# A graph-attention stage: the column groups of its weighted sum take halves of the queries in place of even and odd key blocks

## The chip, the cores and the metric

One core of a Trainium2 chip runs the whole program; seven others are idle. The metric is the device time of one execution in microseconds (us), the median of the executions. Engines: TensorE (PE, its weight loads are listed apart as PEld), VectorE (DVE), ScalarE (ACT), GpSimd (POOL), SyncE (SP, which here only issues DMA).

## What is computed

Four graph layers follow each other on x of 8 graphs x 1024 nodes x 64 features, each behind a layer norm. The change lies in the fourth, and there in its hidden attention:

```
def gat_layer(x, graph, W, b):
    h = x @ W                                  # one head: 64 -> 128
    s = einsum('bnd,bmd->bnm', h, h) * graph
    s = where(s == 0.0, -1e16, s)
    a = softmax(s, axis=2)
    return einsum('bnm,bmd->bnd', a, h) + b
heads = vmap(...)                              # 8 heads
x = leaky_relu(cat(heads), 0.01)               # 8 x 128 = 1024 channels
out = gat_layer(x, graph, W_out, b_out)
```

All is float32. With 8 graphs and 8 heads there are 64 units of work; a unit is one head of one graph. In a unit the kernel uses that a @ (x W) = (a @ x) W: it sums the 64 input features of the keys with the softmax weights (this is z, 64 features for each of 1024 queries), divides by the row sums, and multiplies by the head's W (64 to 128) and by its part of W_out (128 to 64) afterwards.

## The kernel before

`hidden_attention` (L275 to L718) runs for each unit g over 8 tiles t of 128 queries x 1024 keys. The order of each engine is written out by hand in one loop for each engine over g and t; semaphores tie them.

For a tile: PE makes the scores (`score`, L411, four products of 512 columns in a two-pass format), DVE adds the mask and takes the row maximum (`mask_tile`, L547), ACT takes the exponential and the row sum in place (`exp_tile`, L628), DVE turns the tile in 32 x 32 blocks into `weights_t` (`turn_tile`, L556). The scores have two places in PSUM, so `score(i)` waits until tile i - 2 is masked (`masked_ready`); step t of unit g issues the score of tile 8g + t + 2. The ring behind them holds four tiles.

After a unit's eight tiles are turned, its results are made while the next unit's tiles run:

- `values(g-1, part)` (L425), in four parts, at t = 2, 3, 4, 5, behind the score of that step. The keys stand in 32 blocks of 32 (NB = 32, Q = 32). `x_rep` holds the features of a key block repeated on the four groups of 32 partitions, and `weights_t` has, on each group a of 32 partitions, the weights of 256 queries. A product therefore uses 32 rows and 64 columns of the array: row group a of four, and column group c of two. Before the change c = b % 2: even key blocks are summed on partitions 0 to 63 of PSUM and odd ones on 64 to 127, in products of 256 columns; a part is 8 key blocks x 4 row groups = 32 products. A float32 product appears in the profile as two records, each with a weight load of its own, so a part is 64 records.
- `copy_z` (L632, ACT, t = 6) moves the sums out of PSUM as z, 128 x 1024: two half sums, still to be added.
- `normalise` (L693, POOL) multiplies z in place by the inverse row sums `inv_cols`. These come from `invert` (DVE, t = 1), go through memory (`inv_rows`) and come back spread over 128 partitions, in two DMAs on SP (L373, L377).
- `head_out` (L444, PE, t = 0 of the unit after) multiplies by `wz`. Its two products (one for each half of the queries, 512 columns, 128 rows) also add the even and odd sums, since `wz` stands twice, on rows 0 to 63 and 64 to 127. They are four records.
- `activate` (L639, ACT, t = 0, behind `exp_tile` and `copy_y`), then `project_out` (L451, PE, t = 1): `wo` x hidden and `wx` x z, for the two halves of the queries in the two column groups, eight records. `take_out` (ACT) and `add_out` (POOL) follow.

`project(g+2)` (L403), `copy_y`, `round_y` and `split_y` prepare the factor y of the scores of a later unit. Some units have further work on DVE: of each graph's eight units u = 0 to 7, u = 1 and 2 end with `split_rows` (L521), u = 3 and 4 with `find_zero_cols` (L530), both for the next graph, and u = 7 builds its mask (L537, eight times). The last graph has none of it.

## Time and profile before

| | us |
|---|---|
| median of 3 runs | 2781.16 |
| lowest, highest | 2780.2, 2785.39 |
| profiled execution, its time | 2786.11 |
| profiled execution, its span | 2784.3 |
| of it the hidden attention's 64 units, with their tail | about 996 to 2491 |

The profiled execution lies 5 us above the median; 1.8 us lie around its span. Durations below are those of this one execution. A row with "x64" stands for 64 instructions; in rows of the timeline the columns are start, duration, engine, line, operation, output<-input, count, and in brackets how long the engine had been idle and what ended that. PE durations are modelled and include the way through the array, so that two neighbours overlap; the distance between starts is the better measure.

### The profile page before, as it was taken

Reading aid. Unit: us, or ns where it says so; the run is one execution under the profiler, and the core shown is the slowest. Engines: PE = TensorE matmul, PEld = TensorE weight load, DVE = VectorE, ACT = ScalarE, POOL = GpSimd, SP = SyncE. Lnnn points to the kernel's source line nnn. Section 1 sums busy time; section 2 is a strip of 40 time slices with the busy share of each in tenths; the row PEclk is TensorE's granted clock in tenths of the full one; section 3 lists DMA queues with packets and bytes.
Section 4 is the critical chain, followed back from the end, with each engine's and each line's share of the span. In section 5 each row is a group of like instructions: output and inputs, shape, how many; then the busy total and the mean of one; then the engine's idle time right before and its main releaser. Section 6 shows DMA issues by size and latency. Waiting matters only on the chain. (4 is left out here: it accounts for less than half of the span.)

```text
span 2784.3 us, 57963 instructions
## 1 busy us (share of the span) xinstructions
PE 2259.4 (81%) x24510; PEld 1463.7 (53%) x24510; DVE 2234.9 (80%) x2971; ACT 1471.3 (53%) x2331; POOL 602.4 (22%) x351
## 2 busy tenths in 40 slices
PE   3855556667767689999999898998998989968997
PEld 2632234444446555565555555655555556636665
DVE  6569985678874598988988989989889898837775
ACT  2412221369962156566566665665656656636665
POOL 0036662000000012222222222222222222210000
PEclk8968788879988779999999999999999999979999
DMA  2000000000000201010010010100100100010000
GB/s 104 1 0 0 0 0 0 2 1 1 1 2 1 59 23 39 17 47 25 24 40 25 27 38 17 48 25 25 40 25 28 36 17 32 25 47 1 1 1 31
DMA packets 61879, 60.79 MB, mean 22 GB/s; under 512 B 50368, under 2 KB 51520, under 8 KB 60992
## 3 DMA queue, kind: packets, MB, share of 16 engines
q1 hardware_dynamic: 61632, 57.21, 6.6%
q8 instruction: 191, 3.13, 0.5%
q14 instruction: 56, 0.46, 0.1%
HBM read 44.34 MB, written 4.46 MB: 18 GB/s over the span
## 5 line engine op out<-in xcount | busy, mean ns | idle before, releaser
L547 DVE CUSTOM_DVE_ANT_0 x_sb<-ps_score,hid_mask 128x1024 f32<-128x1024 f32 x512 | 616.5, 1204 | 142.4 <-PE ps_score L419 140.3
L628 ACT ACTIVATE x_sb<-x_sb,hid_neg_max 128x1024 f32<-128x1024 f32 x512 | 586.8, 1147 | 268.2 <-DVE hid_neg_max L547 268.1
L556 DVE STREAM_TRANSPOSE hid_weights_t<-x_sb 128x1024 f32<-128x1024 f32 x512 | 631.4, 1233 | 1.3 <-ACT x_sb L628 0.6
L419 PE MATMUL ps_score<-hid_y_hi,hid_xs 128*128 128x512 f32 x1024 | 471.4, 460 | 51.3 <-DVE hid_neg_max L547 47.8
L437 PE MATMUL ps_low<-hid_weights_t,hid_x_rep 32*64 32x256 f32 x16384 | 506.7, 380 | 0.8 <-ACT hid_share L656 0.8
L437 PEld LDWEIGHTS ps_low<-hid_weights_t,hid_x_rep 32*64 32x64 f32 x16384 | 346.2, 131 | 139.9 <-issue 82.3
L419 PE MATMUL ps_score<-hid_y_lo,hid_xs 128*128 128x512 f32 x1024 | 411.2, 402 | 0.0
L697 POOL TENSOR_TENSOR hid_z<-hid_z,hid_inv_cols 128x1024 f32<-128x1024 f32 x64 | 197.9, 3092 | 761.1 <-ACT hid_z L636 761.1
L419 PEld LDWEIGHTS ps_score<-hid_y_hi,hid_xs 128*128 128x128 f32 x1024 | 195.6, 191 | 257.5 <-issue 116.0
L690 POOL TENSOR_TENSOR hid_y_lo<-hid_y_wide,hid_y_hi 128x1024 fp32r<-128x1024 f32 x64 | 153.1, 2392 | 348.5 <-ACT hid_y_wide L623 348.5
L419 PEld LDWEIGHTS ps_score<-hid_y_lo,hid_xs 128*128 128x128 f32 x1024 | 197.1, 192 | 42.9 <-issue 14.6
L447 PE MATMUL ps_low<-hid_z,hid_wz 128*128 128x512 f32 x256 | 134.0, 648 | 38.1 <-POOL hid_z L697 22.2
L636 ACT COPY hid_z<-ps_low 128x1024 f32<-128x1024 f32 x64 | 64.8, 1012 | 143.0 <-PE ps_low L437 143.0
L1788 ACT ACTIVATE hyp_blend_exp<-hyp_blend,hyp_minus_one 128x512 f32<-128x512 f32 x72 | 52.0, 723 | 161.7 <-DVE hyp_blend L1851 161.7
L167 PE MATMUL ps_low<-ident,gat_weights 128*128 128x128 f32 x512 | 80.0, 307 | 61.7 <-ACT gat_weights_t L256 55.6
L537 DVE SCALAR_TENSOR_TENSOR hid_mask<-hid_zero_col,hid_zero_row,adj_mask 128x1024 bf16<-128x1024 bf16 x64 | 111.3, 1748 | 0.0
L167 PEld LDWEIGHTS ps_low<-ident,gat_weights 128*128 128x128 f32 x512 | 64.1, 157 | 85.9 <-issue 43.2
L219 DVE CUSTOM_DVE_ANT_0 out_masked<-ps_score,out_mask 128x1024 f32<-128x1024 f32 x64 | 78.3, 1224 | 27.6 <-issue 22.9
L708 POOL TENSOR_TENSOR h_sb<-h_sb,hid_share 128x512 f32<-128x512 f32 x56 | 72.0, 1285 | 131.4 <-ACT hid_share L656 131.4
L447 PEld LDWEIGHTS ps_low<-hid_z,hid_wz 128*128 128x128 f32 x256 | 46.9, 201 | 97.0 <-POOL hid_z L697 34.5
L643 ACT ACTIVATE hid_hidden<-ps_low,hid_bias_pos 128x1024 f32<-128x1024 f32 x64 | 71.4, 1116 | 49.7 <-PE ps_low L447 48.8
L618 ACT CAST hid_y_hi<-ps_low 128x1024 fp32r<-128x1024 f32 x64 | 65.0, 1016 | 61.8 <-PE ps_low L406 61.8
(308 smaller groups left out, 3810.5 us busy)
## 6 DMA issues: line engine op xcount, KB each, us to landing
hid_inv_cols<-hid_inv_rows SPq DMA_DIRECT2D x64, 512.0 KB, 3.7
hid_x_rep<-h_sb SPq DMA_DIRECT2D x128, 64.0 KB, 2.5
adj_rows<-in_adj SPq DMA_DIRECT2D x8, 512.0 KB, 8.0
x_sb<-in_x SPq DMA_DIRECT2D x2, 1024.0 KB, 6.1
x_saved<-x_sb SPq DMA_DIRECT2D x1, 2048.0 KB, 6.5
x_sb<-x_saved SPq DMA_DIRECT2D x1, 2048.0 KB, 8.0
out_x<-x_sb SPq DMA_DIRECT2D x1, 2048.0 KB, 6.3
hid_inv_rows<-hid_row_inv SPq DMA_DIRECT2D x64, 4.0 KB, 1.4
```

Source lines behind the costliest of these rows:

```text
L167: ins = pe.transpose(m.ps_turn[:, half, k * P:(k + 1) * P], a.weights[:, t % 3, j * P:(j + 1) * P], m.ident[:])
L219: dve.tensor_tensor_reduce(a.masked[:, t % 2, :], scores, mask, -1.0, HUGE, ALU.add, ALU.min, a.neg_max[:, par, t:t + 1]).then_inc(a.maske ...
L419: ins = pe.matmul(m.ps_score[:, i % 2, half * HALF:(half + 1) * HALF], xs[:, g // HEADS % 2, t * P:(t + 1) * P], y[g % 2][k][:, half * HAL ...
L437: ins = pe.matmul(m.ps_low[c * F:(c + 1) * F, a, 0:NT * Q], x_rep[a * Q:(a + 1) * Q, g // HEADS % 2, b, :], weights_t[a * Q:(a + 1) * Q, g ...
L447: ins = pe.matmul(m.ps_low[:, half, :], wz[:, g % HEADS, :], z[:, half * HALF:(half + 1) * HALF], start=True, stop=True)
L537: dve.scalar_tensor_tensor(out=mask[:, t, :], in0=zero_col[:], scalar=zero_row[:, t:t + 1], in1=m.mask[:, t, :], op0=ALU.min, op1=ALU.min) ...
L547: dve.tensor_tensor_reduce(ring[:, i % RING, :], m.ps_score[:, i % 2, :], mask[:, t, :], -1.0, HUGE, ALU.add, ALU.min, neg_max[:, g % 2, t ...
L556: dve.transpose(weights_t[:, g % 2, :, t, :], ring[:, i % RING, :].rearrange("p (b j) -> p b j", j=Q)).then_inc(tile_turned, 1)
L628: act.activation(ring[:, i % RING, :], ring[:, i % RING, :], ACT.Exp, scale=-1.0, bias=neg_max[:, g % 2, t:t + 1], accum_out=row_sum[:, g ...
L690: pool.tensor_tensor(y[g % 2][1][:], y_wide[:], y[g % 2][0][:], ALU.subtract)\
L697: pool.tensor_tensor(rows, rows, inv_cols[:].rearrange("p i t -> p t i"), ALU.mult)\
L708: pool.tensor_tensor(out, out, share[:].rearrange("p (t f) -> p t f", f=F), ALU.add)\
```

## The change

The column group c no longer takes every other key block but one half of the queries that a row group holds: 128 of its 256 columns. Each key block is now multiplied twice, with c = 0 and c = 1, in products of 128 columns, and each accumulates over all 32 key blocks. A part has 64 products (128 records, each with its weight load) in place of 32 (64 records). z then is 128 x 512: partitions 0 to 63 hold the first 512 queries and 64 to 127 the others, and nothing remains to be added. So `copy_z` and `normalise` handle half the elements, `inv_cols` is half as large and filled by two DMAs of 64 partitions, `head_out` and the `wx` products of `project_out` use 64 rows for each half of the queries in place of 128.

```diff
-        inv_cols = sb("inv_cols", [P, P, NT])
-        z = sb("z", [P, N])
+        inv_cols = sb("inv_cols", [P, P, NT // 2])
+        z = sb("z", [P, HALF])
...
-                sp.dma_start(inv_rows[g % 2], row_inv[:, g % 2, :]).then_inc(inv_stored, 16)
+                sp.dma_start(inv_rows[g % 2].rearrange("c p t -> p c t"),
+                             row_inv[:, g % 2, :].rearrange("p (c t) -> p c t", c=2)).then_inc(inv_stored, 16)
...
-                sp.dma_start(inv_cols[:].rearrange("p i t -> p (i t)"),
-                             inv_rows[g % 2].rearrange("(a p) t -> a (p t)", a=1).to_broadcast([P, N]))\
-                    .then_inc(inv_spread, 16)
+                for c in range(2):
+                    sp.dma_start(inv_cols[c * F:(c + 1) * F, :, :].rearrange("p i t -> p (i t)"),
+                                 inv_rows[g % 2, c:c + 1].rearrange("a p t -> a (p t)")
+                                 .to_broadcast([F, HALF])).then_inc(inv_spread, 16)
...
                 for b in range(part * NB // 4, (part + 1) * NB // 4):
-                    c = b % 2
                     for a in range(P // Q):
-                        ins = pe.matmul(m.ps_low[c * F:(c + 1) * F, a, 0:NT * Q],
-                                        x_rep[a * Q:(a + 1) * Q, g // HEADS % 2, b, :],
-                                        weights_t[a * Q:(a + 1) * Q, g % 2, b, :, :],
-                                        start=(b == c), stop=(b == NB - 2 + c))
+                        for c in range(2):
+                            ins = pe.matmul(m.ps_low[c * F:(c + 1) * F, a, 0:NT // 2 * Q],
+                                            x_rep[a * Q:(a + 1) * Q, g // HEADS % 2, b, :],
+                                            weights_t[a * Q:(a + 1) * Q, g % 2, b,
+                                                      c * NT // 2:(c + 1) * NT // 2, :],
+                                            start=(b == 0), stop=(b == NB - 1))
...
                 for half in range(2):
-                    ins = pe.matmul(m.ps_low[:, half, :], wz[:, g % HEADS, :],
-                                    z[:, half * HALF:(half + 1) * HALF], start=True, stop=True)
+                    rows = slice(half * F, (half + 1) * F)
+                    ins = pe.matmul(m.ps_low[:, half, :], wz[rows, g % HEADS, :], z[rows, :],
+                                    start=True, stop=True)
...
-                for k, (weight, src) in enumerate(((wo, hidden), (wx, z))):
-                    for half in range(2):
-                        ins = pe.matmul(m.ps_low[half * F:(half + 1) * F, 0, :], weight[:, g % HEADS, :],
-                                        src[:, half * HALF:(half + 1) * HALF],
-                                        start=(k == 0), stop=(k == 1))
+                for half in range(2):
+                    pe.matmul(m.ps_low[half * F:(half + 1) * F, 0, :], wo[:, g % HEADS, :],
+                              hidden[:, half * HALF:(half + 1) * HALF], start=True, stop=False)
+                for half in range(2):
+                    rows = slice(half * F, (half + 1) * F)
+                    ins = pe.matmul(m.ps_low[rows, 0, :], wx[rows, g % HEADS, :], z[rows, :],
+                                    start=False, stop=True)
...
-                act.copy(z[:].rearrange("p (t a j) -> p a t j", t=NT, a=P // Q),
-                         m.ps_low[:, :, 0:NT * Q].rearrange("p a (t j) -> p a t j", j=Q)).then_inc(z_ready, 1)
+                act.copy(z[:].rearrange("p (t a j) -> p a t j", t=NT // 2, a=P // Q),
+                         m.ps_low[:, :, 0:NT // 2 * Q].rearrange("p a (t j) -> p a t j", j=Q))\
+                   .then_inc(z_ready, 1)
...
-                rows = z[:].rearrange("p (t i) -> p t i", t=NT)
+                rows = z[:].rearrange("p (t i) -> p t i", t=NT // 2)
                 pool.tensor_tensor(rows, rows, inv_cols[:].rearrange("p i t -> p t i"), ALU.mult)\
                     .then_inc(z_normed, 1)
```

No instruction changes its place among the others of its engine. On PE, a stretch with two parts of the weighted sum (`ps_low<-hid_weights_t`) between the scores of two tiles reads, before the change:

```order
L437 MATMUL ps_low<-hid_weights_t,hid_x_rep 64x256 x32
L419 MATMUL ps_score<-hid_y_hi,hid_xs 128x512
L419 MATMUL ps_score<-hid_y_lo,hid_xs 128x512
L419 MATMUL ps_score<-hid_y_hi,hid_xs 128x512
L419 MATMUL ps_score<-hid_y_lo,hid_xs 128x512
L437 MATMUL ps_low<-hid_weights_t,hid_x_rep 64x256 x32
```

and with the change, where line 437 has become 439 and line 419 has become 421:

```order
L439 MATMUL ps_low<-hid_weights_t,hid_x_rep 64x128 x64
L421 MATMUL ps_score<-hid_y_hi,hid_xs 128x512
L421 MATMUL ps_score<-hid_y_lo,hid_xs 128x512
L421 MATMUL ps_score<-hid_y_hi,hid_xs 128x512
L421 MATMUL ps_score<-hid_y_lo,hid_xs 128x512
L439 MATMUL ps_low<-hid_weights_t,hid_x_rep 64x128 x64
```

The products of a part have doubled in number and halved in columns; what stands around them is the same.

## Rows read from the trace of the kernel before

**Rows 1.** The page: busy time of each engine, share of the span, instructions.
```profile
PE 2259.4 (81%) x24510; PEld 1463.7 (53%) x24510; DVE 2234.9 (80%) x2971; ACT 1471.3 (53%) x2331; POOL 602.4 (22%) x351
```

**Rows 2.** Waits from 996 to 2457 us: who waited for whom, total, times, longest.
```profile
DVE x_sb L547 <- PE ps_score L419: 140.3, 241, 1.1
...
PEld ps_low L447 <- POOL hid_z L697: 25.4, 27, 1.1
```

**Rows 3.** Timeline: two steps with a part of the weighted sum.
```profile
1603.04 0.40 PE L419 MATMUL ps_score<-hid_y_lo,hid_xs 128*128 128x512 f32 x1
1603.36 1.53 PEld L437 LDWEIGHTS ps_low<-hid_weights_t,hid_x_rep 32*64 32x64 f32 x64 [0.36 <-issue]
1603.37 1.98 PE L437 MATMUL ps_low<-hid_weights_t,hid_x_rep 32*64 32x256 f32 x64
1603.47 1.22 DVE L547 CUSTOM_DVE_ANT_0 x_sb<-ps_score,hid_mask 128x1024 f32<-128x1024 f32 x1 [0.65 <-PE ps_score L419]
...
1606.40 1.98 PE L437 MATMUL ps_low<-hid_weights_t,hid_x_rep 32*64 32x256 f32 x64
```

**Rows 4.** Short stretches of one part, line 437: length, PE busy (records in it), clock, DMA.
```profile
1600.32:1600.38 0.06, 0.06 (x8) 1.00 0.73 158
1600.38:1600.59 0.21, 0.21 (x8) 1.00 0.97 235
1600.59:1600.65 0.06, 0.06 (x16) 1.00 1.27 337
```

**Rows 5.** Timeline and line 393: 128-column products in two column groups.
```profile
1609.56 1.09 PE L393 MATMUL ps_low<-ident,h_sb 128*64 128x128 f32 x16
...
L393 PE MATMUL ps_low<-ident,h_sb x256: 272/273/475, 974.5 to 2166.2; 128*64 128x128 f32 x128
```

**Rows 6.** Groups by line and shape: busy us, mean ns, idle before and its releasers.
```profile
L697 POOL TENSOR_TENSOR hid_z<-hid_z,hid_inv_cols 128x1024 f32<-128x1024 f32 x64 | 197.9, 3092 | 761.1 <-ACT hid_z L636 761.1
L447 PE MATMUL ps_low<-hid_z,hid_wz 128*128 128x512 f32 x256 | 134.0, 648 | 38.1 <-POOL hid_z L697 22.2 <-DVE hid_zero_col L530 12.9 <-DVE hid_xs L521 3.1
L636 ACT COPY hid_z<-ps_low 128x1024 f32<-128x1024 f32 x64 | 64.8, 1012 | 143.0 <-PE ps_low L437 143.0
L656 ACT COPY hid_share<-ps_low 128x512 f32<-128x512 f32 x56 | 32.9, 587 | 57.8 <-PE ps_low L455 57.8
L708 POOL TENSOR_TENSOR h_sb<-h_sb,hid_share 128x512 f32<-128x512 f32 x56 | 72.0, 1285 | 131.4 <-ACT hid_share L656 131.4
```

**Rows 7.** Timeline around head_out and activate, a unit with split_rows before it.
```profile
1614.82 1.00 ACT L623 COPY hid_y_wide<-ps_low 128x1024 f32<-128x1024 f32 x1
...
1615.88 1.12 ACT L643 ACTIVATE hid_hidden<-ps_low,hid_bias_pos 128x1024 f32<-128x1024 f32 x1
```

**Rows 8.** The same with find_zero_cols before it.
```profile
1636.48 1.98 PE L447 MATMUL ps_low<-hid_z,hid_wz 128*128 128x512 f32 x4 [0.92 <-DVE hid_zero_col L530]
...
1638.50 1.12 ACT L643 ACTIVATE hid_hidden<-ps_low,hid_bias_pos 128x1024 f32<-128x1024 f32 x1 [0.76 <-PE ps_low L447]
...
1642.77 1.22 DVE L547 CUSTOM_DVE_ANT_0 x_sb<-ps_score,hid_mask 128x1024 f32<-128x1024 f32 x1 [0.57 <-PE ps_score L419]
```

**Rows 9.** The same in a unit with neither.
```profile
2376.41 1.12 ACT L643 ACTIVATE hid_hidden<-ps_low,hid_bias_pos 128x1024 f32<-128x1024 f32 x1 [0.33 <-PE ps_low L447]
```

**Rows 10.** Timeline of the tail, from the last turned tile on.
```profile
2457.77 2.85 POOL L697 TENSOR_TENSOR hid_z<-hid_z,hid_inv_cols 128x1024 f32<-128x1024 f32 x1 [11.38 <-ACT hid_z L636]
...
2460.68 2.71 PE L447 MATMUL ps_low<-hid_z,hid_wz 128*128 128x512 f32 x4 [4.10 <-POOL hid_z L697]
...
2463.43 1.11 ACT L643 ACTIVATE hid_hidden<-ps_low,hid_bias_pos 128x1024 f32<-128x1024 f32 x1 [4.60 <-PE ps_low L447]
...
2480.31 3.78 PE L447 MATMUL ps_low<-hid_z,hid_wz 128*128 128x512 f32 x4 [4.08 <-POOL hid_z L697]
```

**Rows 11.** PE in stretches of the tail: busy (records), granted clock, DMA.
```profile
2461.00:2465.00 4.00, 2.80 (x6) 0.60 0.43 132
...
2481.00:2485.00 4.00, 3.09 (x4) 0.50 0.00 0
```

More of the change, by code:

```diff
@@ L311, in hidden_attention @@
         share = sb("share", [P, HALF])
-        inv_rows = nc.dram_tensor("hid_inv_rows", (2, P, NT), F32).ap()
+        inv_rows = nc.dram_tensor("hid_inv_rows", (2, 2, P, NT // 2), F32).ap()
         gram_ready = sem("gram_ready")
@@ L383, in _ @@
                     load_rows(g // HEADS + 1)
-            sp.wait_ge(inv_spread, 16 * UNITS)
+            sp.wait_ge(inv_spread, 32 * UNITS)
         @block.tensor
@@ L694, in normalise @@
                 pool.wait_ge(z_ready, g + 1)
-                pool.wait_ge(inv_spread, 16 * (g + 1))
-                rows = z[:].rearrange("p (t i) -> p t i", t=NT)
+                pool.wait_ge(inv_spread, 32 * (g + 1))
+                rows = z[:].rearrange("p (t i) -> p t i", t=NT // 2)
                 pool.tensor_tensor(rows, rows, inv_cols[:].rearrange("p i t -> p t i"), ALU.mult)\
```

## The prediction

> **What bounds the kernel now.** The page first: PE and DVE are each busy four fifths of the span, ACT and POOL far less [rows 1]. So the question in each stretch is which of PE and DVE waits for the other. The list of waits answers it for the 64 units: DVE waited for scores 241 times, 140 us in all, 0.58 us each [rows 2]. The timeline shows where: in the four steps that carry a part of the weighted sum, the step takes 3.04 us (1603.37 to 1606.40), PE has no pause in it beyond the change of product kind, and DVE sits idle 0.65 us before each mask [rows 3]. In these steps PE sets the time, in all others DVE does. The exception are the eight units that build masks (u = 7) and half of those behind them, where DVE has work enough everywhere. So 241 steps of 512 are PE's, and there a nanosecond more or less in a part is one on the path.
>
> The start of this PE-bound stretch is set by another chain: z is normalised, head_out, activate, project_out, then the score of t = 2 and the first part. Every nanosecond by which project_out ends earlier moves the whole PE-bound stretch, since DVE idles in it.
>
> **Values (the heart of it).** How PE runs a part now: eight records start within 0.06 us, none in the next 0.21 us, then eight more (the count in the next stretch goes to 16, since the first eight still flow), and so on [rows 4]. Eight are the eight combinations of row and column group; they stream side by side, and a new eight comes when they are through, every 0.216 us (1.98 less one duration of 0.374 is 1.61 us, for seven such steps, the first weight load and 0.05 us from first to last of eight [rows 3]). With 128 columns: line 393 has products of 128 columns in two column groups, 16 records in 1.09 us; less one duration of 0.273 and the first load of 0.05, that is 0.77 us for seven steps of a pair, 0.109 us each [rows 5]. So a step of half the columns takes half the time, and its weight load still hides behind the record before it. A part of the changed kernel has 128 records, 16 steps of eight: 15 x 0.109 + 0.10 = 1.74 us to its last start, and that record then streams 0.107 in place of 0.213 us. Now 1.61 + 0.21 = 1.82, then 1.74 + 0.11 = 1.85: I take **+0.02 us** a part, and 241 x 0.02 = **+5 us**. Bounds: what this needs is a record each 13.6 ns over 1.7 us. The trace shows eight within 0.06 us (7 ns each, so one engine start is no limit) but never more than 64 in 1.7 us (27 ns each). From below, the two steps cannot be shorter than their columns: -0.02, -5 us. From above, 27 ns each would be 3.46 us a part, +1.6 us, +390 us. I take the low end, because the 27 ns have a cause in the rows: eight records start at once and then nothing starts for 0.21 us, which is waiting for the columns and not for records; and the pairs of line 393 halve their step when the columns halve.
>
> The Trainium skill's page "TensorE: Matmul & The Clock Gate" (section "Wait — 56ns, not 53.3ns?") says that start-to-start never drops below about 25 ns however small the product is. By that a part would take 128 x 25 ns = 3.2 us, an estimate from the page, and the kernel would come out some 330 us slower. Against it stand the eight starts in 0.06 us in different groups of the array; for it, that no row has sustained more than one in 27 ns.
>
> **The rest of z.** copy_z writes 512 elements a partition in place of 1024: 1.01 us becomes 0.59 (line 656, same shape) [rows 6]. normalise: 3.09 becomes about 1.5; line 708 with 512 elements takes 1.29, which is the floor [rows 6]. head_out: four records of 512 columns follow each other, 0.43 us each (1.98 us with a duration of 0.59 and a load of 0.1) [rows 8]; with 64 rows each, the two halves lie in different row groups and run side by side, as the four row groups of a part do, so 4 x 0.43 becomes 2 x 0.43, **-0.86 us**. project_out: wo is unchanged; the wx pair ran in two column groups and still does, so two steps remain two steps. What is new is a change of the array's division in the middle. Its price from a row: the last score record starts at 1603.04 and streams 0.23 us (the distance of such records), so it is through at 1603.27; the first load of the part stands at 1603.36, and 0.05 us more go to that load, which is not ahead of time [rows 3]. So **+0.14 us**, on the path, between 0 and 0.2. The Trainium skill's page "TensorEngine Tiling (Array Packing)" (section "Key Properties") says that changing the tiling mode drains the engine, and the row agrees with 0.09 us of pause.
>
> What of this reaches the end depends on activate, which on ACT stands behind copy_y and waits for head_out. Three kinds of unit:
> - With split_rows before it: activate starts 0.06 us after copy_y, without a wait [rows 7]. Nothing is gained; the 0.14 us are lost. 7 graphs x 2 = 14 units: **+2.0 us**.
> - With find_zero_cols before it: head_out starts late for DVE's sake (0.92 us, in total 12.9, hence 14 times [rows 6, 8]), activate waits 0.76 us for it, and 0.06 of that remains behind copy_y. 0.70 - 0.14 = 0.56 us, x 14 = **-7.9 us**.
> - With neither: head_out waits for normalise (27 times [rows 2]), activate waits 0.33 us [rows 9]. normalise and copy_z together are 2 us earlier, so head_out starts with its score, and ends early: 0.27 - 0.14 = 0.13 us. Of the 27, seven are in the mask-building units, where DVE hides it. 20 x 0.13 = **-2.6 us**.
> The gain is at most what DVE idles at t = 2 and after (0.57 and 4 x 0.65 us [rows 8, 3]), so all of it counts.
>
> **The tail.** Behind the last tile everything is one chain, twice: copy_z, normalise, head_out, activate, project_out [rows 10]. Each time copy_z gives 0.43 and normalise 2.85 / 2 = 1.42 us. The first head_out takes 2.75 us (2460.68 to 2463.43) because the granted clock drops in it (mean 0.60, between full and half [rows 11]); 1.85 us earlier it lies before the drop and has half the steps: about 1.05, -1.7 us. The second runs at half clock (0.50, that is 1.2 GHz): four steps of 0.85 become two, -1.7. Less two changes of division, 0.2 each: 2 x 1.85 + 3.4 - 0.4 = **-6.7 us**. Between -4.5 and -8.5, by where the clock falls.
>
> **Without effect.** The two DMAs that fill inv_cols carry half the bytes each and are issued one behind the other on SP, where nothing waits behind them but the loads of the next graph's rows; normalise sat idle 11 to 12 us before copy_z ended and never waited for inv_cols (all 761 us of its wait are copy_z's [rows 6]). If the smaller pieces of the store cost even 3 us it is hidden. PE's program grows by 64 x 4 x 128 instructions; were its supply late, that would be the first rival.
>
> **Sum.** +5.0 + 2.0 - 7.9 - 2.6 - 6.7 = -10.2 us against the span of 2784.3: 2774.1. The profiled execution (2786.1) lies 5 us over the median, so it goes on the median: 2781.2 - 10.2 = **2771.0 us**, 0.4% faster. What a measurement of this kernel can tell from no change is about 0.2%, 5.6 us.
>
> **Rivals.**
> 1. *Records come too slowly* (slower). The engine can't sustain a record with its load each 13.6 ns. From 13.6 ns on each nanosecond costs 128 ns a part, 31 us over 241 parts. At 17 ns: 0.44 us a part, +100 us, 2870; at the 27 ns that are all that was ever sustained: +390 us, 3160. For it: never seen. Against it: rows 4 and 5 as above. Chance 0.14, most of it at the mild end.
> 2. *The row groups open one after another* (slower). The new order puts both halves of a row group (four records) in front of the next one. If PE takes records strictly in order and the second record of one group blocks those behind it, a key block costs 4 x (0.109 + 0.013) = 0.49 in place of 0.218 us, a part 3.9 us, +2.1 us, +500 us, 3270. Against it: eight starts in 0.06 us [rows 4] can only be, with two records to each product, if records pass waiting ones even now. Chance 0.06.
> 3. *It comes to nothing* (within 0.2%). The parts lose 0.04 us in place of 0.02, the division changes cost 0.2 in head_out too, and the tail's clock falls elsewhere: -10.2 + 5 + 3 + 2 = 0, 2781. Each of the three is within its bounds. Chance 0.20.
> 4. *My forecast*, -6 to -20 us: 0.60. The far end is parts at -0.02 us.
>
> Chances: faster 0.60, same 0.20, slower 0.20. The range 2760 to 2798 takes in forecast and rival 3, and of rival 1 what costs up to 17 us (14.1 ns a record); outside lie about 0.2.
>
> **What would show it.** In the changed kernel's timeline: a part of 128 records in 1.95 us, the step still 3.05 us, DVE idle 0.65 us in it. Rival 1 shows a part of 2.2 to 3.5 us, DVE idle 1 us and more; rival 2 one of 4 us. L447 successor: four records, two and two, 1.1 us from first start to last end in place of 1.98. Its wait for POOL is gone. activate's wait of 0.76 and 0.33 us is gone. project_out ends 0.14 us later behind activate. The tail (2457 to 2490) is 6 us shorter. I am wrong in the main thing if the parts change by more than 0.05 us either way.

## The result, and the profile after

The changed kernel takes 2899.11 us (median of 4), the kernel before 2783.27 us in the same comparison: 1.0415 times as long, interval 1.0395 to 1.0435. The prediction was 2771 us, faster; even its range, up to 2798, is missed by 100 us. The profiled execution has a span of 2896.5 us, 112.2 more than before. In this comparison and in those below every execution lies close to its median except one: one of the six of e13 took 6441 us, and its ratio leaves that one out.

The page of the changed kernel: busy times, and the queue that brings instructions.

```profile
PE 2299.6 (79%) x40894; PEld 1574.0 (54%) x40894; DVE 2221.2 (77%) x2971; ACT 1441.7 (50%) x2331; POOL 503.4 (17%) x351
...
q8 instruction: 319, 5.23, 0.8%
```

The same queue on the page of the kernel before (packets, MB, share of 16 DMA engines):

```profile
q8 instruction: 191, 3.13, 0.5%
```

PE's busy time grew by 40 us only [rows 1], though it has 32,768 more instructions (records and loads). They come in 128 more packets of 16 KB, so a packet holds 256 instructions.

The waits of the changed kernel (total, times, longest), against 140.3 us in 241 times of [rows 2]; the second row is PE's loads in the parts waiting for nothing that a semaphore shows:

```profile
DVE x_sb L553 <- PE ps_score L421: 251.4, 207, 3.4
...
PEld ps_low L439 <- issue: 181.0, 403, 2.2
```

The timeline, the first three parts of one unit, to be laid beside [rows 3]:

```profile
1714.69 2.10 PE L439 MATMUL ps_low<-hid_weights_t,hid_x_rep 32*64 32x128 f32 x128
...
1717.84 0.67 PE L439 MATMUL ps_low<-hid_weights_t,hid_x_rep 32*64 32x128 f32 x27
...
1719.35 1.77 PE L439 MATMUL ps_low<-hid_weights_t,hid_x_rep 32*64 32x128 f32 x101 [0.84 <-issue]
...
1722.17 0.66 PE L439 MATMUL ps_low<-hid_weights_t,hid_x_rep 32*64 32x128 f32 x23
...
1722.28 1.23 DVE L553 CUSTOM_DVE_ANT_0 x_sb<-ps_score,hid_mask 128x1024 f32<-128x1024 f32 x1 [1.94 <-PE ps_score L421]
...
1723.09 1.81 PE L439 MATMUL ps_low<-hid_weights_t,hid_x_rep 32*64 32x128 f32 x105 [0.27 <-issue]
```

Here are both causes of the loss. The first part is whole: 2.10 us against 1.98, its step 3.15 us against 3.04. The second breaks off after 27 records; for 0.8 us PE has nothing in flight and waits for nobody ("issue"), then come the other 101. The third breaks after 23. From here on, "first to last" means from the start of a part's first record to the start of its last, and a hole is a distance of over 0.3 us between two starts in a part. All 252 parts of the kernel before take 1.61 us first to last, without a hole. In the changed kernel a part that nothing holds up takes 1.83 us (68 of them), and 126 of 252 have a hole (87 us in all, the longest 2.7); the mean is 2.29 us.

The start of the whole part, in short stretches (length, PE busy and records in flight in it, then loads, clock, DMA), beside [rows 4]:

```profile
1714.69:1714.80 0.11, 0.11 (x8) 0.11 (x16) 1.00 0.37 11
1714.80:1714.91 0.11, 0.11 (x16) 0.11 (x24) 1.00 0.85 24
...
1716.00:1716.20 0.20, 0.20 (x34) 0.20 (x26) 1.00 0.00 0
```

In it four groups of eight start as forecast (the last three 0.109 us apart, within a group 6.7 ns from record to record); after these come mostly single starts, about 16.5 ns apart, in two streams that overlap.

The groups of the z side and of the masks (busy, mean ns, idle before), beside [rows 6]:

```profile
L704 POOL TENSOR_TENSOR hid_z<-hid_z,hid_inv_cols 128x512 f32<-128x512 f32 x64 | 99.3, 1552 | 880.1 <-ACT hid_z L642 880.1
...
L451 PE MATMUL ps_low<-hid_z,hid_wz 64*128 64x512 f32 x256 | 74.2, 657 | 26.6 <-DVE hid_zero_col L536 17.4 <-DVE hid_xs L527 4.6 <-POOL hid_z L704 4.6
...
L642 ACT COPY hid_z<-ps_low 128x512 f32<-128x512 f32 x64 | 37.5, 586 | 229.2 <-PE ps_low L439 228.9
```

They do what was forecast: normalise goes from 3.09 to 1.55 us, copy_z from 1.01 to 0.59, and head_out's four records take 1.13 us in place of 1.98; head_out waits for POOL 5 us in all, no longer 22.

The clearest rows stand in the tail, where the last unit's whole sum runs with no scores between (before: 256 records in one piece, 7.17 us):

```profile
2575.80 2.42 PE L439 MATMUL ps_low<-hid_weights_t,hid_x_rep 32*64 32x128 f32 x151 [0.78 <-ACT hid_share L663]
2579.88 2.08 PE L439 MATMUL ps_low<-hid_weights_t,hid_x_rep 32*64 32x128 f32 x128 [1.66 <-issue]
2583.90 3.01 PE L439 MATMUL ps_low<-hid_weights_t,hid_x_rep 32*64 32x128 f32 x128 [1.94 <-issue]
2587.64 3.27 PE L439 MATMUL ps_low<-hid_weights_t,hid_x_rep 32*64 32x128 f32 x105 [0.73 <-issue]
2590.98 0.58 ACT L642 COPY hid_z<-ps_low 128x512 f32<-128x512 f32 x1 [15.32 <-PE ps_low L439]
```

The pieces break off 128 records apart: 128 records with their 128 loads are one packet of 256 instructions. The packets' work starts 4.0 and 3.7 us apart. Between 1000 and 2400 us of the changed kernel the two closest instruction packets start 3.28 us apart; a step with a part wants a little more than one (264 instructions) and should take 3.05 us.

The trace shows the same in the middle of the kernel. If all PE instructions in it (82,345) are numbered in the order of their starts, every one of the 129 holes (126 in parts, three in the tail) ends at the 137th or 138th of a block of 256, that is always at the same place of a packet; so do all holes of e1, e3, e6, e11 and e14 (29 to 141 in each). A packet's own record ends 1.2 to 1.6 us before the hole does (nine in ten, median 1.40). And in 47 of the 48 units outside u = 7 and 0 the first part, which follows four steps without a part, is whole: the same instructions run at full pace where the supply had time to get ahead.

### The profile page after: what moved, and what is told of

The parts are those of the page before. It is cut to its first block and busy times, and to the rows that moved or that the text cites. A ratio compares the mean times of both kernels' runs of the same rounds, so it can differ in the third digit from the quotient of the medians.

```text
span 2896.5 us, 90795 instructions
## 1 busy us (share of the span) xinstructions
PE 2299.6 (79%) x40894; PEld 1574.0 (54%) x40894; DVE 2221.2 (77%) x2971; ACT 1441.7 (50%) x2331; POOL 503.4 (17%) x351
## 5 line engine op out<-in xcount | busy, mean ns | idle before, releaser
L439 PE MATMUL ps_low<-hid_weights_t,hid_x_rep 32*64 32x128 f32 x32768 | 601.7, 276 | 59.7 <-issue 56.6
L439 PEld LDWEIGHTS ps_low<-hid_weights_t,hid_x_rep 32*64 32x64 f32 x32768 | 500.2, 131 | 189.4 <-issue 181.0
L421 PE MATMUL ps_score<-hid_y_hi,hid_xs 128*128 128x512 f32 x1024 | 449.9, 439 | 49.2 <-DVE hid_neg_max L553 42.3
L704 POOL TENSOR_TENSOR hid_z<-hid_z,hid_inv_cols 128x512 f32<-128x512 f32 x64 | 99.3, 1552 | 880.1 <-ACT hid_z L642 880.1
L642 ACT COPY hid_z<-ps_low 128x512 f32<-128x512 f32 x64 | 37.5, 586 | 229.2 <-PE ps_low L439 228.9
L167 PE MATMUL ps_low<-ident,gat_weights 128*128 128x128 f32 x512 | 79.8, 306 | 61.7 <-ACT gat_weights_t L256 55.6
L458 PE MATMUL ps_low<-hid_hidden,hid_wo 128*64 128x512 f32 x256 | 70.8, 632 | 40.7 <-ACT hid_hidden L650 39.5
L543 DVE SCALAR_TENSOR_TENSOR hid_mask<-hid_zero_col,hid_zero_row,adj_mask 128x1024 bf16<-128x1024 bf16 x64 | 100.4, 1577 | 0.0
L634 ACT ACTIVATION_READ_ACCUMULATOR x_sb<-x_sb,hid_neg_max 128x1 f32 x512 | 97.0, 189 | 0.0
L249 ACT ACTIVATE out_weights<-out_masked,out_neg_max 128x1024 f32<-128x1024 f32 x64 | 73.5, 1149 | 46.8 <-DVE out_neg_max L219 46.2
L451 PE MATMUL ps_low<-hid_z,hid_wz 64*128 64x512 f32 x256 | 74.2, 657 | 26.6 <-DVE hid_zero_col L536 17.4
```

The lines of the kernel that those rows point to most:

```text
L167: ins = pe.transpose(m.ps_turn[:, half, k * P:(k + 1) * P], a.weights[:, t % 3, j * P:(j + 1) * P], m.ident[:])
L249: act.activation(a.weights[:, t % 3, :], a.masked[:, t % 2, :], ACT.Exp, scale=-1.0, bias=a.neg_max[:, par, t:t + 1], accum_out=a.row_sum[ ...
L421: ins = pe.matmul(m.ps_score[:, i % 2, half * HALF:(half + 1) * HALF], xs[:, g // HEADS % 2, t * P:(t + 1) * P], y[g % 2][k][:, half * HAL ...
L439: ins = pe.matmul(m.ps_low[c * F:(c + 1) * F, a, 0:NT // 2 * Q], x_rep[a * Q:(a + 1) * Q, g // HEADS % 2, b, :], weights_t[a * Q:(a + 1) * ...
L451: ins = pe.matmul(m.ps_low[:, half, :], wz[rows, g % HEADS, :], z[rows, :], start=True, stop=True)
L543: dve.scalar_tensor_tensor(out=mask[:, t, :], in0=zero_col[:], scalar=zero_row[:, t:t + 1], in1=m.mask[:, t, :], op0=ALU.min, op1=ALU.min) ...
```

## Experiments

**Theory A**: PE's instructions arrive too slowly, one packet of 256 in 3.3 us or more, 13 ns an instruction. **Rivals**: B, the halves of 128 columns, their order or their number cost the array time; C, the columns or the array's handling of each record set it. As one measure for all, the stretch of a unit from the first record of its first part to the last start of its fourth (with three scores between; the mean over units, without those whose sum runs in u = 7 or 0): before, 536 PE instructions in 10.73 us; changed, 1048 in 13.23 us (11.67 to 16.18), 12.6 ns an instruction.

**Twice the records, nothing else (e1).** The kernel before, each product in two of 128 columns that follow in the same tile of the array.

```diff
-                        ins = pe.matmul(m.ps_low[c * F:(c + 1) * F, a, 0:NT * Q], ...)
+                        for s in range(2):
+                            ins = pe.matmul(m.ps_low[c * F:(c + 1) * F, a, s * NT // 2 * Q:(s + 1) * NT // 2 * Q], ...)
...
```

> The kernel before, with each product of the weighted sum issued as two products of 128 columns of the same column group: records and weight loads as many as in the changed kernel, everything else (z of full size, key blocks even and odd) as before. Theory A, instruction supply: blocks of 16 KB (256 instructions) reach PE no faster than one in about 3.3 us, and a step with a part now needs 264 and more; holes of 0.3 to 2 us with nothing issued appear in the parts, as in the changed kernel, and the time is that of the changed kernel plus what the smaller z gives, 2899 + 8 to 14 = 2905 to 2920 us. Rival B, the order of the row groups or the query halves are at fault: no holes, 2780 to 2800 us.

2995.76 us, ratio 1.0751 (1.0733 to 1.0769). Twice the records are enough to do the damage, but not as expected, and both theories missed the time: the clean part is 2.55 us, and only 30 parts have a hole (22 us). Stretch 14.61 us: 13.9 ns an instruction, so the supply nearly follows. An added record costs (2.55 - 1.61) / 64 = 14.7 ns here, against 3.4 in the changed kernel. Here four records in a row go to one tile (one row group with one column group), there two; whether that order is the reason was not shown, and e11 below, whose added records change tile, pays about as much.

**The smaller z with the long products (e2).** The changed kernel, but each key block as before in one product of 256 columns, even and odd blocks apart; their addition is left out.

```diff
+                    c = b % 2
-                        for c in range(2):
-                            ins = pe.matmul(m.ps_low[c * F:(c + 1) * F, a, 0:NT // 2 * Q], ...)
+                        ins = pe.matmul(m.ps_low[c * F:(c + 1) * F, a, 0:NT * Q], ...)
```

> The changed kernel with the products of the kernel before (256 columns, even and odd key blocks); the adding of even and odd sums is left out, and z, normalise, head_out and wx handle half of it. It shows what the smaller z gives by itself. My sum of the prediction without the parts: -2.0 ... that is +2.0 - 7.9 - 2.6 - 6.7 = -15 us, so 2768 us; the parts as before (64 records in 1.98 us). Rival: project_out's two kinds of product cost more than head_out gives, 2780 us or above.

2756.38 us, 0.9895 (0.9878 to 0.9911); span 31.0 us less than before. Parts as before. So z gives 31 us, twice my sum, and what the 64 more records a part cost is 112.2 + 31.0 = 143 us.

**The order (e3).** The changed kernel, column groups outside and row groups inside, as the eight of the kernel before.

```diff
-                    for a in range(P // Q):
-                        for c in range(2):
+                    for c in range(2):
+                        for a in range(P // Q):
```

> The changed kernel with the loops over row group and column group exchanged (four row groups of one column group, then four of the other), the same products. Theory A, instruction supply: within 0.5% of the changed kernel, 2885 to 2913 us, with the same holes. Rival B, two products of one row group in a row hold up those behind them: parts as short as 1.95 us and 2780 to 2800 us.

2907.19 us, 1.0442 (1.0424 to 1.0459), an interval that overlaps the changed kernel's: no gain. Clean part 1.83 us, holes in 138 parts. The order of the row groups is not the cause.

**Empty instructions (e5).** The kernel before with four nops behind each product, each raising a semaphore.

```diff
+                        for filler in fillers:
+                            pe.nop().then_inc(filler, 1)
```

> The kernel before with four empty PE instructions (each only counts up a semaphore of its own) behind each product of the weighted sum: as many instructions as in the changed kernel, but products, columns and weight loads as before. Theory A, instruction supply: the holes appear all the same, 2880 to 2920 us. Rival C, what limits is the array's handling of records and weight loads, not the number of instructions: at most a few ns for each, no holes, 2785 to 2800 us.

7206.17 us, 2.5869 times, far outside both expectations. In the timeline the next product starts only when the records before the nops have about ended; 32,768 nops cost 4420 us, 135 ns each, with the granted clock down to 0.63 on average. Packets then come 17 us apart and more: the run says nothing on the supply.

**An eighth of the columns (e9).** The number of instructions is kept and the array's work taken away.

```diff
-                            ins = pe.matmul(m.ps_low[c * F:(c + 1) * F, a, 0:NT // 2 * Q],
+                            tiles = NT // 2 if b == 0 else 1
+                            cols = Q if b == 0 else 16
+                            ins = pe.matmul(m.ps_low[c * F:(c + 1) * F, a, 0:tiles * cols],
...
```

> The changed kernel with the same 128 records a part (the same number of PE instructions), but each product of a key block other than the first streams 16 columns in place of 128; the weighted sum of the other columns is left out. So the array has an eighth of the work. Theory A (PE's instructions come too slowly: blocks of 256 instructions, never closer than about 3.3 us in the changed kernel's trace, so some 13 ns an instruction): the step with a part has 264 to 270 instructions and still takes 3.4 us and more on average, holes with nothing issued stay in the parts, and the time is 2820 to 2880 us, near the 2899 of the changed kernel. Rival B (each record start costs PE its 14 to 17 ns, and the holes belong to the products in the array): clean parts of about 1.8 us remain, the holes go, 2750 to 2780 us. Rival C (columns set all of it): a part takes under 1 us, DVE never waits for scores, 2620 to 2660 us.

3005.91 us, 1.079 (1.0744 to 1.0836): outside every expectation, not under the changed kernel but above it, because the granted clock fell (mean 0.79 against 0.92), which lengthens the scores. The stretch is 13.50 us (11.69 to 16.16) against the changed kernel's 13.23, but the two can't be compared: the changed kernel's ran at full clock, these at a mean of 0.63 to 0.91, where a step without a hole takes up to 3.91 us, 2.63 at full clock. What can be compared are the holes: 105 parts have them, 119 us in all. Timeline:

```profile
2613.26 1.75 PE L441 MATMUL ps_low<-hid_weights_t,hid_x_rep 32*64 32x16 f32 x128
2616.06 0.30 PE L441 MATMUL ps_low<-hid_weights_t,hid_x_rep 32*64 32x16 f32 x6
2617.40 1.38 PE L441 MATMUL ps_low<-hid_weights_t,hid_x_rep 32*64 32x16 f32 x122 [1.04 <-issue]
2619.84 0.39 PE L441 MATMUL ps_low<-hid_weights_t,hid_x_rep 32*64 32x16 f32 x2
2621.15 1.96 PE L441 MATMUL ps_low<-hid_weights_t,hid_x_rep 32*64 32x16 f32 x126 [0.92 <-issue]
```

The holes belong to the number of instructions, not to the array's work, and all but one of them end at the same place of a block of 256 as in the changed kernel. Rivals B and C fall for the holes. What stands of a price of the record itself: a whole part took 1.37 us at full clock (10.7 ns a record) and 1.72 at half.

**Half the records (e4).** The changed kernel with one 128-column product for each key block and row group; the other half of the columns is left out.

```diff
-                        for c in range(2):
+                    c = b % 2
```

> The changed kernel, but with one product for each key block and row group as in the kernel before (even blocks in one column group, odd ones in the other), of 128 in place of 256 columns; so 64 records a part, and half of the columns of the weighted sum is left out. Theory A (supply of instructions): a step with a part has some 200 instructions, 2.6 us of supply, less than DVE needs; no holes, the part takes about 0.9 us from first to last start (8 steps of 0.109 us), DVE does not wait for scores, 2610 to 2650 us. Rival B (128-column products in themselves start badly, whatever their number): parts of 1.3 us and more with holes, 2690 to 2760 us. Against the run with 128 records of 16 columns this one has eight times the columns a record and half the records.

2604.18 us, 0.9347 (0.9328 to 0.9365). (A step has 136 PE instructions; the expectation's 200 was miscounted.) Four parts have holes, 4 us; stretch 7.87 us. DVE's wait for scores is gone from the list. The same 128-column products, half as many, are harmless. Within a part they start as densely as in the changed kernel (64 in 0.94 us, 14.7 ns each), but a step of 2.27 us asks for 136 instructions, 16.7 ns each, in place of 264.

```profile
1697.50 1.21 PE L439 MATMUL ps_low<-hid_weights_t,hid_x_rep 32*64 32x128 f32 x64
...
1699.77 1.21 PE L439 MATMUL ps_low<-hid_weights_t,hid_x_rep 32*64 32x128 f32 x64
```

**Three quarters (e14).** The changed kernel with 96 records a part; a quarter of the keys is left out.

```diff
-                for b in range(part * NB // 4, (part + 1) * NB // 4):
+                for b in range(part * 6, (part + 1) * 6):
...
```

> The changed kernel with six key blocks a part in place of eight: 96 records in place of 128, 16 products of two 128-column halves left out of the weighted sum in each part (a quarter of the keys). From the first record of the first part to the last of the fourth there are 792 PE instructions in place of 1048. Theory A (a supply of 12.6 ns an instruction, which is what 1048 in 13.2 us were, with 128 columns as with 16): 792 x 12.6 = 10.0 us; the array alone needs 4 x 1.38 + 3 x 1.46 = 9.9. So holes are rare (under 30 parts, under 20 us in all) and the stretch takes 9.9 to 10.6 us, less than the 10.73 of the kernel before with 64 long records: 2700 to 2745 us. Rival (each 128-column record brings its share of the holes): 3/4 of 127 parts and of 92 us, 2760 to 2790 us.

2725.97 us, 0.9778 (0.9763 to 0.9792), as theory A says; stretch 10.36 us, inside its 9.9 to 10.6. Holes in 47 parts and 33 us, more than the 30 parts and 20 us it allowed, half of the rival's 95 parts and 69 us. So the limit sets in gradually: the shortest stretch (9.50 us) has 12.0 ns an instruction, the mean one 13.1, and a unit in which a packet comes late shows it. Its tail shows the same size of piece with another program:

```profile
2410.56 2.42 PE L439 MATMUL ps_low<-hid_weights_t,hid_x_rep 32*64 32x128 f32 x151 [0.78 <-ACT hid_share L663]
2414.12 2.08 PE L439 MATMUL ps_low<-hid_weights_t,hid_x_rep 32*64 32x128 f32 x128 [1.14 <-issue]
2417.87 1.81 PE L439 MATMUL ps_low<-hid_weights_t,hid_x_rep 32*64 32x128 f32 x105 [1.66 <-issue]
```

151 and 128 again, though its parts have 96 records: this program is shorter by 16,384 instructions, 64 whole packets, so the packets end at the same place of the last sum.

**Tiny records added to the kernel before (e11).**

```diff
...
+                    for k in (b - 1, b):
+                        for a in range(P // Q):
+                            ins = pe.matmul(m.ps_low[k % 2 * F:(k % 2 + 1) * F, a, 0:16], ...)
...
```

> The kernel before with its 64 records a part unchanged, and behind each two key blocks the same eight products once more with 16 of the 256 columns (these columns are then counted twice in the weighted sum). So the PE instructions of the changed kernel (128 records a part) come with the z side and the long products of the kernel before, and the array's work grows by 16 columns in 256, 6%. Theory A (supply): blocks of 256 instructions come no closer than 3.3 us, a step with a part has 264 instructions and more, so it takes 3.4 us on average in place of 3.04, with holes in a third to a half of the parts: 2870 to 2930 us, as the changed kernel plus its saving on z. Rival B (something in the two 128-column halves themselves, or in four records of one row group in a row): no holes, a part takes 1.61 us + 8 short steps of 0.05 to 0.1 us, +0.1 to +0.2 us in place of holes: 2810 to 2840 us.

2984.68 us, 1.072 (1.0704 to 1.0736): both theories missed. A clean part takes 2.60 us, not 1.7: eight long records and eight tiny ones take 0.325 us, eight long ones 0.216, so each added record costs (2.60 - 1.61) / 64 = 15.5 ns though it has 16 columns. At 13.9 ns an instruction (stretch 14.56 us) the supply nearly follows, and only 26 parts have holes (19 us). Theory A is thus not the whole: a second price is paid by the record itself, and here, as in e1, it hides the first.

**Five parts in place of four (e6 from the changed kernel, e7 from the one before).**

```diff
-                for b in range(part * NB // 4, (part + 1) * NB // 4):
+                for b in range(part * NB // 5, (part + 1) * NB // 5):
...
-                    if 2 <= t < 6 and 1 <= g <= UNITS:
+                    if 2 <= t < 7 and 1 <= g <= UNITS:
...
```

> The changed kernel with the weighted sum of a unit in five parts (behind the scores of t = 2 to 6, six or seven key blocks each) in place of four, and the turning of the next graph's rows behind the last part moved from t = 6 to t = 7. Theory A (supply): a step with a part has some 240 instructions, 3.15 us of supply, against 3.45 before; five such steps take 15.7 us where four and one without a part took 14.4 + 2.4 = 16.8; holes get rarer, DVE waits less; 60 units by 0.8 to 1.1 us: 2830 to 2860 us. Rival B (the holes belong to the array and come with each part, whatever stands around it): as many holes as before or more (five parts), and each clean step 2.8 us; 2860 to 2900 us.

> The kernel before with its weighted sum in five parts at t = 2 to 6 in the same way. A step with a part had 3.04 us and 0.65 us of DVE idle; with four fifths of a part it has 2.72 us (1.61 / 5 = 0.32 less), the fifth one in place of a 2.4 us step. Five of 2.72 and none of 2.4: 13.6 against 4 x 3.04 + 2.4 = 14.6 us, 1.0 us a unit by some 55 units: 2725 to 2740 us if the longer way of z (its last part is one tile later) is hidden; 2760 to 2790 if head_out then comes late. Theory A adds: some 187 instructions a step, no holes in either case.

e6: 2869.23 us, 1.0308 (1.0289 to 1.0327). The holes fell from 87 to 54 us, in 83 of 314 parts, as a thinner stream of instructions (200 to 232 a step; the 240 written there was too many) lets the supply follow more often. e7: 2823.3 us, 1.0133 (1.0113 to 1.0153), slower where I expected faster. The fifth part ends a tile later and z with it; `head_out` waits for POOL 36 times, 55.6 us, with the score of t = 1 behind it: DVE idles 0.9 to 1.4 us before that tile's mask in u = 1, 4, 5 and 6, where it did not idle before. **e8** (from e7) and **e10** (from e6) were to move ACT's copy of z out of the way:

```diff
...
+                    if t == 7 and 1 <= g <= UNITS:
+                        copy_z(g - 1)
                     if g < UNITS:
                         exp_tile(g * NT + t)
...
-                    if t == 6 and 1 <= g <= UNITS:
-                        copy_z(g - 1)
-                    if t == 6 and n < B and u in (1, 2):
+                    if t == 7 and n < B and u in (1, 2):
```

> The kernel before with the weighted sum in five parts, and ACT's copy of z (and its rounding of the next rows) moved from behind exp of t = 6 to ahead of exp of t = 7, so that ACT no longer waits for the fifth part (it waited 295 us for it against 143 with four). Theory (the loss of 38 us was ACT's wait): DVE idles 0.33 us in five steps in place of 0.65 in four, less what PE waits for z's copy in t = 7: 2745 to 2775 us. Rival (z's way is one tile longer whatever ACT does, and PE's project and turning of rows stand behind it): 2790 to 2830 us.

> The changed kernel with the weighted sum in five parts and ACT's copy of z moved in the same way. Against the version with five parts without that move (2869 us) it should give back what ACT waits: if that is as in the kernel before, 30 to 50 us, 2820 to 2840. The holes of a slow instruction supply stay as they are with five parts (60 us in 109 parts), so theory A expects it to stay above the kernel before; if it falls under 2786 the supply would not be what holds the change back.

2816.86 (1.0119) and 2861.18 us (1.0289). The edit was a slip: behind exp of t = 6 and ahead of exp of t = 7 are the same place in ACT's order, so only the rounding of the rows moved. ACT waited 294.7 us for the fifth part as in e7 (294.6). Neither theory was tested; that an extra part can pay with z's way shortened stays open.

**Where do z's 31 us come from? (e12)** Unit by unit (each from its mask of t = 2 to the next unit's), e2 against before: u = 2, 3 with split_rows ahead -2.6 us in all (forecast +2), u = 4, 5 with find_zero_cols ahead -10.5 (forecast -7.9), u = 1 and 6 -4.6 (forecast -2.6), the two chains of the tail -5.7 (forecast -6.7), u = 0 +2.5, and u = 7, of which I said "DVE hides it", -8.9. (How much falls to u = 0 and how much to u = 7 depends on where a unit is said to begin; their sum is -6 to -9.) In u = 7 of the kernel before, in the timeline of POOL and DVE:

```profile
1147.70 2.38 POOL L690 TENSOR_TENSOR hid_y_lo<-hid_y_wide,hid_y_hi 128x1024 fp32r<-128x1024 f32 x1 [1.77 <-ACT hid_y_wide L623]
...
1148.45 2.72 DVE L537 SCALAR_TENSOR_TENSOR hid_mask<-hid_zero_col,hid_zero_row,adj_mask 128x1024 bf16<-128x1024 bf16 x1
...
1163.88 1.27 DVE L537 SCALAR_TENSOR_TENSOR hid_mask<-hid_zero_col,hid_zero_row,adj_mask 128x1024 bf16<-128x1024 bf16 x1
...
1166.20 2.95 POOL L697 TENSOR_TENSOR hid_z<-hid_z,hid_inv_cols 128x1024 f32<-128x1024 f32 x1 [13.09 <-ACT hid_z L636]
...
1167.35 2.88 DVE L537 SCALAR_TENSOR_TENSOR hid_mask<-hid_zero_col,hid_zero_row,adj_mask 128x1024 bf16<-128x1024 bf16 x1
```

A building of the mask takes 1.27 us, but where POOL is at work it ends 1.1 us behind the end of POOL's instruction (1150.08 and 1151.17; 1169.15 and 1170.23): it waits for it. All 22 buildings that start under an instruction of POOL end 1.08 or 1.09 us behind it, whether they take 2.3 or 3.4 us. e12 halves normalise alone:

```diff
-                rows = z[:].rearrange("p (t i) -> p t i", t=NT)
+                rows = z[:].rearrange("p (t i) -> p t i", t=NT)[:, 0:NT // 2, :]
```

> The kernel before, but POOL normalises only the first 512 of z's 1024 columns (the division by the row sum is left out for the others); all else is as before. Theory (POOL's normalise disturbs DVE's building of the mask where they fall together: 2.8 us in place of 1.27 for one of the eight in 7 of the graphs): one building of a mask in each u = 7 takes 1.27 us, 7 x 1.4 = -9.8 us; in the tail 2 x 1.6 = -3.1; units where head_out waited for POOL 0 to -0.3 us each: in all -13 to -20 us, 2762 to 2770. Rival (those instructions are slow for a reason of their own, and the 30 us of the smaller z came from copy_z or head_out): -3 to -8 us, 2773 to 2780.

2767.81 us, 0.9949 (0.9934 to 0.9965), in the theory's range. The instruction that took 2.88 us takes 1.45; normalise alone brings 15 us, about half of z's gain. The Trainium skill's page "SBUF — State Buffer" (section "Who interferes with whom") says that a DVE instruction with two SBUF inputs and a GpSimd instruction that reads SBUF lock each other out for the whole instruction, whichever came first. The rows agree where POOL's instruction came first, and DVE's mask_tile, whose one input is in PSUM, keeps its 1.20 us beside POOL. POOL waiting for DVE is not shown.

**The masks moved out of the way (e13).** The kernel before with nothing left out of it; only the place of the buildings changes.

```diff
                     if n < B and u == HEADS - 1:
-                        build_mask(n, t)
+                        for k in {2: (0, 1), 3: (2, 3), 4: (4, 5), 6: (6, 7)}.get(t, ()):
+                            dve.wait_ge(masked_ready, g * NT + k + 1)
+                            build_mask(n, k)
```

> The kernel before; only the eight buildings of the next graph's mask on DVE in u = 7 are issued at other steps: two each behind the masks of t = 2, 3, 4 and 6 in place of one in each step, so that none falls on POOL's split_y (t = 0 and 7) and normalise (t = 5). Theory (a building of the mask waits for POOL's instruction to end before it starts: 2.72 of which 1.64 overlap, 2.88 of which 1.79, 2.28 of which 1.20, against 1.27 alone): up to 1.5 + 1.6 + 1.0 = 4.1 us in 7 graphs, 29 us; as the moved ones may meet POOL's other work in one or two places, 2755 to 2770 us. Rival (PE or ACT holds u = 7 as soon as DVE is faster, or the POOL work moves along with it): 2775 to 2785 us.

2766.70 us, 0.9930 (0.9917 to 0.9943): 0.7% faster than the kernel before and 4.6% faster than the changed one, in the theory's range. All 56 moved buildings now take 1.3 us, what they take alone; of the 64 in the row (busy us, mean ns) only one of the first graph, which did not move, still takes 3.4. The mean was 1748 ns before:

```profile
L537 DVE SCALAR_TENSOR_TENSOR hid_mask<-hid_zero_col,hid_zero_row,adj_mask 128x1024 bf16<-128x1024 bf16 x64 | 81.1, 1313 | 0.0
```

## Why the prediction was wrong

**The step that failed** is the choice in the part on values: "I take the low end, because the 27 ns have a cause in the rows ... which is waiting for the columns and not for records". With it the parts stood in the sum at +5 us; by e2 they cost 143. That reading of [rows 4] was right for the kernel before: there the columns did set the time. It was no evidence for the supply. Eight starts in 0.06 us show how fast instructions already in the queue can start; the rows held no stretch in which 128 records followed each other, and [rows 5] had 16. A bound of +390 us from the only rate ever sustained stood beside the term, and I took the end that needed a rate never seen. Two things were in it:

- *Records in a part.* First to last 1.74 us forecast for a whole part, 1.83 measured. The shorter stream of the last record does give 0.10 back, as I had it (from it to the next part 1.32 us in place of 1.42), so the step of a whole part is 3.15 against 3.04 us: +0.11 in place of +0.02. Over 224 steps (56 units, four each; the seven that build masks hide theirs) that is an estimate of +25 us; I had +5 over 241.
- *Supply.* The remark that the program "grows by 64 x 4 x 128 instructions; were its supply late, that would be the first rival" named the cause and gave it no price. The mean step with a part is 3.61 us (before 3.05); less the 0.11 above that is 0.45 us, over 224 steps some +100 us. It is more than the holes over 0.3 us hold (87), so some of it must be smaller waits: only 67 of 189 steps had a part of 1.83. That those too are the supply's is likely but not shown. And in the tail the last sum takes 15.1 us in place of 7.2: +7.9.

Together 25 + 100 + 8 = 133 of the 143 us that e2 gives as the price of the records, as an estimate; the other 10 were not located.

**Rival 1** was right in kind and near in price. It said 31 us for each nanosecond over 13.6: the mean part of 2.29 us is 17.9 ns a record, +133 us, which on top of 2771 makes 2904, and 2899 was measured. That it comes so near is partly luck: the records cost 10 us more than this, the tail among them, and z gave 16 us more than my sum. I put its "17 ns, 2870" at the mild end of a chance of 0.14. The range's upper end, too, was reckoned wrong: from 2771 to 2798 are 27 us, 14.5 ns a record, not "17 us (14.1 ns a record)". Rival 2 is refuted by the clean parts of 1.83 us, in the changed kernel and in e3, and rival 3 by the result. The Trainium skill's page "TensorE: Matmul & The Clock Gate", which the prediction set aside, pointed the right way, but not by the floor that it states: starts came 7 ns apart in a burst and 14.3 in a whole part, so no floor of 25 ns held between starts. That 524 records took 13.23 us over the stretch, 25.2 ns each, is no evidence for it either: e14 gives 26.2 and e1 27.9, and the stretch has holes in it. The Trainium skill's page "Runtime: NRT & Kernel Launch" (section "Instruction fetch mechanics") states blocks of 16 KB, 256 instructions, as the rows show, and adds that the fetching is hidden since instructions are dispatched more slowly than they are filled in; here it was not hidden.

**The terms of z** gave -31 us in place of -15.2. The units behind split_rows, +2.0: measured -2.6; the change of the array's division did lengthen project_out by 0.14 us (1.94 to 2.08 from its first start to its end), as forecast, but DVE's wait at t = 2 shrank from 0.30 to 0.17 all the same, for a reason that was not tested (head_out is shorter by 0.85 us, and the score of t = 1 stands behind it). The units behind find_zero_cols, -7.9: measured -10.5. Those with neither, -2.6: -4.6. Tail -6.7: the two chains from copy_z to the end of add_out's input took 2.5 and 3.3 us less, -5.7; the first head_out did not escape the half clock (2.08 us, not 1.05). What was missed is the wait of DVE for POOL, -9 in u = 7: "seven are in the mask-building units, where DVE hides it" took an engine's time as fixed.

**What would show it** was right: "Rival 1 shows a part of 2.2 to 3.5 us".

Not settled: why packets keep 3.3 us and more apart. The trace shows the round, not its reason. A hole ends mostly 2.3 to 2.9 us after the start of the last packet before it (about 1 us under way, then 1.4). Where one late packet followed another (55 times), the second started no sooner than 1.05 us after the first instruction of the one before it had begun to run (median 1.15). Together that is some 3.6 us for 256 instructions, as if the next packet were asked for only when the one before is at work. And the price of a record beyond its columns (10.7 ns at best in e9, 14.3 in the changed kernel, 15.5 for an added one in e11) was measured, not explained.

## What to carry to other kernels

Count PE's instructions (loads too) against the time of the stretch in which they stand. Here the changed kernel, whose stretches ran at 12.6 ns an instruction, had holes in 126 of 252 parts, at 13.1 (e14) in 47, at 13.9 (e1, e11) in 30 and 26, at 14.7 (e4) in 4 and at 20 (before) in none, whatever the array could have done. Splitting products to save work elsewhere then cost more (143 us) than it saved (31). A rate seen in a burst is no rate that lasts; if the change needs one that no row of sufficient length shows, the far bound is the forecast until shown otherwise. And an engine's instruction time is not fixed: look at one kind in all its places, and where it doubles, see who else was at work.

## What the runs showed of the hardware

- Packets of 256 PE instructions, never closer than 3.2 us in any run (3.22 us in e11, 3.28 in the changed kernel). The changed kernel's stretches had 12.6 ns an instruction on average, its last sum 14.7 (1024 in 15.1 us). There, with nothing between, the packets' work started 3.7 to 4.0 us apart.
- Every hole in the changed kernel's parts ended at the same place of a block of 256 instructions, and a median of 1.40 us after a packet had ended.
- Less work in the array lowered the clock: with 16 columns in place of 128 the mean grant fell from 0.92 to 0.79 and the kernel got slower (3006 against 2899 us), with PE shown as busy for 80% of the span. A whole part of it took 1.37 us at full clock and 1.72 at half.
- A nop that raises a semaphore cost PE 135 ns behind a product (e5, with the granted clock at 0.63).
- A bf16 operation on DVE with two SBUF inputs waited for POOL's instruction to end: 2.88 us for 1.27, and all 22 that started under one ended 1.08 or 1.09 us behind it.
